# A linear-attention and mixture-of-experts layer: the expert stage's PE order built around the arriving gathers

## The reference

```python
x = L0_attn_x                                   # (2, 1024, 128) float32: 2048 tokens of 128
x = _layernorm(x + _L0_attn_ref(x, ...))        # linear attention, 16 heads of 8, with its own norm and residual
x = _layernorm(x + _L0_ffn_ref(x, ...))
# _L0_ffn_ref, E = 14 experts, one expert for each token:
logits = x @ router_w
assignments = argmax(logits); weights = softmax(logits)[assignment]
hid = gelu(x @ w1[e] + b1[e])                   # 128 -> 256
sel = hid @ w2[e] + b2[e]                       # 256 -> 128, only the chosen expert counts
moe_out = sel * weights
```

## Time and profile before

| | us |
|---|---|
| median of 3 runs | 109.59 |
| lowest, highest | 108.51, 110.13 |
| the profiled execution's own time | 107.97 |
| its span, first to last instruction | 106.2 |
| outside the span | 1.77 |

### The profile page before, as it was taken

One profiled execution on the slowest core, in us unless ns is written; L12 is line 12 of the kernel. 1 busy time (PEld: TensorE's weight loads), 2 busy tenths in 40 slices (PEclk: granted clock), 3 DMA queues, 4 the chain that ended last, 5 costly groups with the idle time before them and its releaser, 6 DMA issues.

```text
span 106.2 us, 2176 instructions
## 1 busy us (share of the span) xinstructions
PE 80.2 (76%) x588; PEld 68.5 (65%) x588; DVE 64.0 (60%) x258; ACT 58.4 (55%) x180; POOL 63.3 (60%) x109
## 2 busy tenths in 40 slices
PE   5729999999999697662888969998999999620000
PEld 3428698988978596441657769986997989510000
DVE  4699957785639887895001324333478887788500
ACT  0415499467559899970035537655446797804200
POOL 6747899910002396923777776750077888877770
PEclk9999999999999999975599999999999999975555
DMA  2848999600000000540688678770000011111110
GB/s 40 302 163 233 365 320 292 176 11 2 0 0 0 3 6 0 199 169 30 224 260 256 204 206 259 231 207 12 0 0 25 31 52 36 39 49 52 49 49 25
DMA packets 9674, 12.16 MB, mean 114 GB/s; under 512 B 1426, under 2 KB 7230, under 8 KB 9662
## 3 DMA queue, kind: packets, MB, share of 16 engines
q1 hardware_dynamic: 8276, 9.69, 28.2%
q0 software_dynamic: 1024, 2.11, 7.1%
q10 hardware_dynamic: 362, 0.23, 1.1%
HBM read 6.07 MB, written 2.11 MB: 77 GB/s over the span
## 4 chain that ended last, share of the span: by engine, by line
PE 34%; POOL 19%; DVE 13%; DMA 12%; issue 10%; ACT 5%; ACTq 2%; POOLq 1%; DVEq 0%
POOL out L529 11%; DMA acc<-x_rows,source 8%; PE ps_q L1015 7%; PE ps_a L1015 6%; PE ps_o L1015 6%; POOL acc L510 5%; DMA vec_rows<-L_ffn_b 4%; PE ps_r L1015 4%; PE ps_k L1015 4%; POOL rstd L382 3%; PE ps_t L1025 3%; ACT hid L692 2%; DVE acc L965 1%; POOLq L70 1%; ACT k_parts L697 1%
## 5 line engine op out<-in xcount | busy, mean ns | idle before, releaser
L510 POOL DMA_INDIRECT acc<-x_rows,source x16 | 16.2, 1014 | 8.7 <-DVE source L894 3.8
L965 DVE SCALAR_TENSOR_TENSOR acc<-ps_o,share,acc 128x128 f32 x29 | 10.2, 351 | 17.7 <-PE ps_o L1015 15.6
L1015 PE MATMUL ps_o<-w_sb,hid 128*128 x116 | 19.3, 289 | 1.1 <-ACT hid L692 1.0
L529 POOL DMA_INDIRECT out<-k_parts,source x16 | 15.9, 996 | 4.3 <-issue 3.7
L382 POOL TENSOR_TENSOR rstd<-ve,exponent 128x4 f32<-128x4 f32 (+3 forms) x14 | 12.5, 896 | 9.4 <-DVE ve L1003 7.1
L1015 PEld LDWEIGHTS ps_o<-w_sb,hid 128*128 128x128 f32 x116 | 15.3, 190 | 2.6 <-issue 2.1
L692 ACT ACTIVATE hid<-ps_q,shared 128x128 f32<-128x128 f32 x30 | 9.3, 361 | 5.5 <-PE ps_q L1015 5.5
L697 ACT ACTIVATE k_parts<-acc,shift,rstd 128x128 f32<-128x128 f32 x15 | 7.0, 488 | 8.5 <-DVE shift L987 8.4
L692 ACT ACTIVATE hid<-ps_k,shared 128x128 f32<-128x128 f32 x28 | 8.7, 361 | 5.4 <-PE ps_k L1015 4.3
L1015 PE MATMUL ps_q<-xs_t,shared 128*128 (+1 forms) x60 | 10.3, 295 | 0.4 <-ACT xs_t L687 0.4
L1015 PE MATMUL ps_k<-xs_t,shared 128*128 x56 | 9.6, 294 | 0.6 <-ACT xs_t L687 0.6
(11 more groups left out here) (205 smaller groups left out, 195.9 us busy)
## 6 DMA issues: line engine op xcount, KB each, us to landing
shared<-w_sb SPq DMA_DIRECT2D x29, 129.0 KB, 2.3
w_sb<-L_ffn_w SPq DMA_DIRECT2D x1, 1792.0 KB, 7.7
x_rows<-rows SPq DMA_DIRECT2D x4, 258.0 KB, 2.1
x_sb<-L_attn_x SPq DMA_DIRECT2D x4, 256.0 KB, 4.4
acc<-x_rows,source POOLq DMA_INDIRECT x16, 3.2
out<-k_parts,source POOLq DMA_INDIRECT x16
wqkv_sb<-L_attn_Wqkv ACTq DMA_DIRECT2D x1, 192.0 KB, 4.2
wo_sb<-L_attn_Wout SPq DMA_DIRECT2D x1, 64.0 KB, 4.9
```

What stands on the lines that cost most here:

```text
L510: pool.indirect_dma_start(acc[:, t, :], None, x1_rows, bass.IndirectOffsetOnAxis(ap=source[:, t:t + 1], axis=0), bounds_check=last_token, ...
L529: pool.indirect_dma_start(out_rows, bass.IndirectOffsetOnAxis(ap=source[:, t:t + 1], axis=0), res[:, t, :], None, bounds_check=last_token, ...
L965: dve.scalar_tensor_tensor(out=tile, in0=ps_y[j % 2], scalar=share[:].rearrange("p t e -> p (t e)")[:, bass.ds(t_of[j] * ROW + j, 1)], in1 ...
L1015: return pe.matmul(o, l, r, start=start, stop=stop)
```

## The change

PE's order becomes, for tile k: turn k, output of step k-2, hidden of step k. ACT copies a tile ahead of the gelu of the step before it. The fillers ahead of the stage go from 18 to 12, and `owned()` moves behind the register load on DVE. The last tiles (14 and 15) and the steps after them are written out.

```diff
@@ scalar
             tile_t(0)
-            gelu(0, 0)
-            tile_t(1)
-            tile_t(2)
             for j in range(NP):
-                if j + 1 < NP:
-                    gelu(j + 1, (j + 1) % U)
-                if j + 3 < NT:
-                    tile_t(j + 3)
-                for t in APPLY_AFTER.get(j, ()):
+                if j < E - 1:
+                    tile_t(j + 1)
+                gelu(j, j % U)
+                if E - 1 <= j < NT - 1:
+                    tile_t(j + 1)
+                for t in APPLY_AFTER.get(j - 1, ()):
                     apply(t)
+            for t in APPLY_AFTER[NP - 1]:
+                apply(t)
@@ vector
             sources()
-            owned()
 
             dve.wait_ge(steps_ok, 2)
             t_of = tiles(dve)
+            owned()
@@ tensor
-            keep_busy(idle_r, 18)
-            turn(0)
-            hidden(0)
-            turn(1)
-            turn(2)
-            for j in range(NP):
+            keep_busy(idle_r, 12)
+            for k in range(E):
+                turn(k)
+                if k >= 2:
+                    output(k - 2)
+                hidden(k)
+            output(E - 2)
+            turn(E)
+            output(E - 1)
+            hidden(E)
+            turn(E + 1)
+            output(E)
+            hidden(E + 1)
+            for j in range(E + 1, NP):
                 if j + 1 < NP:
                     hidden(j + 1)
-                if j + 3 < NT:
-                    turn(j + 3)
                 output(j)
```

## The result

The changed kernel takes 109.28 us (median of 4 runs, 108.67 to 110.29), the kernel before 109.05 (4 runs, 107.98 to 110.13), and the ratio is 1.014 with an interval of 1.007 to 1.021. The forecast was 107.6, faster. A second comparison of the same kernel gave 1.012 (1.005 to 1.020; 109.73 of 10 runs against 108.87 of 25).

What follows compares the result with a forecast made beforehand. The end was taken to stand at a fixed distance behind POOL's power 2, set by add 16; order 1.9 plus gathers 0.3 less late landing 0.2 saves 2.0, taking 109.59 to 107.6, range 106.2 to 109.2.

Steps and rivals of the forecast that it cites:

- A step without a wait takes 1.11 on PE: PE's step in the expert stage: 0.11 turn, 0.50 output, 0.50 hidden, read from the profile before.
- Turn 13 at 70.48 as before: Start of the forecast's chain on PE: turn 13 unmoved, then copy until 71.05 and hidden 13 at 71.09.
- The forecast's list of signs: What the profile after would show if right: add 16 near 77.8, POOL idle about 1 us ahead of power 2.
- Order, 1.9: PE's new order: two outputs and one hidden pass ahead of the last gather, add 16 earlier by 1.9, lower bound 1.5.
- The gelus take half back: Rival: late landing on gather 13 or 14, or a longer hidden, gelu, output chain; 108.4, chance 0.2.
- The gathers, +0.33: POOL's gather 11 and the four behind it start 0.33 earlier as copy 7 comes sooner; gain 0 to 0.33.
- Late landing: A gather landing about 4 us after issue may fall on gather 13 or 14; 0.2 taken off, bounds 0 and 0.9.
- Fillers, 0: Six fewer fillers ahead of the stage let turn 0 start at 52.9, not 53.85, hidden by the gathers; worth 0.
- the rival of a falling clock: Rival: PE's short gaps and fewer fillers lower the granted clock between 60 and 70 us; 110.2, chance 0.06.
- `owned()` on DVE, 0, and gather 0: `owned()` behind the load ends between 51.8 and 52.9, costing DVE 0; gather 0 gains 0, bounds 0 and 0.67.
- The 0.67 of the rival: Rival: POOL was held by `owned()`, so gather 0 and all others start 0.67 earlier; 106.9, chance 0.15.
- POOL stays last: Tail: POOL remains last to be ready, smallest slack 0.8 at power 5, so the 2.0 carry on to the end.

Runs made afterwards that it cites:

- e1: Changed kernel with hidden's wait for the copied tile moved onto its first matrix instruction, behind the address register work; 1.000 of before, median 108.27.
- e4: Changed kernel with each tile's hidden layer one turn later (turn k, hidden k-1, output k-2); 0.991 of before, 108.52.
- e10: Changed kernel with hidden one turn later and the address work ahead of the copy wait, on chip 2; 0.980 of before, 107.08.
- e11: Changed kernel with POOL waiting for the copy of tile t-6 instead of t-4, on chip 2; 1.005 of before, 108.93.
- e5: e1 with hidden 15 ahead of output 14, on chip 7; 0.999 of before, 113.72 against 114.1.
- e2: Kernel before, old order, with 12 fillers for 18 and `owned()` behind the register load; 0.988 of before.
- e14: Same kernel as e2 measured a second time, 12 runs; 1.000 of before, 109.09 against 109.02.
- e12: Kernel before with 28 instead of 16 warm-up matmuls at its start, on chip 2; 0.982 of before, median 108.61 against 108.87.
- e3: Changed order alone: changed kernel with 18 fillers and `owned()` ahead of the load; 1.018 of before, 109.35.
- e8: Changed kernel with POOL waiting for the copy of tile t-6 instead of t-4, on chip 7; 1.030 of before.
- e15: Same kernel as e10, hidden one turn later and early address, on chip 9; 0.993 of before.

## Why the prediction was wrong

**The step that failed: "A step without a wait takes 1.11 on PE", and with it "Turn 13 at 70.48 as before".** The 1.11 was measured in an order in which each hidden layer had its copy long before. In the new order a step contains turn, copy, address and hidden layer one after the other, 0.31 + 0.27 + 0.25 + 0.54 = 1.37. The forecast had this chain in its hand for turn 13 (copy until 71.05, hidden at 71.09) and did not ask whether it holds for every step. Asking would not have been enough: by its own numbers the chain closes in 0.57 + 0.04 + 0.50 = 1.11, below the 1.30 of the gathers. The term that it had wrong is the hand-over from copy to hidden, taken as 0.04 and measured as 0.25 (to the first matrix instruction); with 0.09 in its place (e1) the step is 1.17 and PE catches up again. A gather comes every 1.30, so a PE that needs 1.37 never catches up once gather 5 has made it late; at 1.11 it would have. From turn 6 to turn 13 it took 9.56 (before 8.51), and from gather 0 to turn 13 22.15 (before 20.85). e1 shortens the loop's address part by 0.16 and seven steps by 1.32; e4 and e10 take the copy out of it, and seven steps take 8.08 and 7.65; e11 takes the gathers' waits for recent copies out and leaves 9.55. These runs show the loop as the cause of the late turn 13. The longer waits behind turn 13, below, are read from the timeline; of them only the exchange in e5 was tried.

The distance from the forecast, add 16 at 77.99 (79.99 less 2.0), to the measured 80.72 is 2.73: 0.28 for the later start, 1.43 for turn 13 beyond that (forecast 70.35 with the gathers' 0.33 and the 0.2 for the late landing, measured 72.06; 1.05 of it is the slower pace from turn 6 to turn 13), and 1.13 behind turn 13 (8.66 for a forecast 7.53), less the 0.1 by which the sum took 1.9 for 1.98 (and roundings). The forecast's list of signs puts add 16 near 77.8, its sum at 77.99.

- *Order, 1.9.* The part that was meant to be gained is there and is small. Turn 13 to add 16 took 9.51 before and 8.66 after: 0.85 gained, where the same pieces were forecast to gain 1.98. The hand-overs were set too low: output 13 came 2.33 behind turn 13 (forecast 2.00; 0.21 of the 0.33 is the address), and each hidden, gelu and output 2.09 and 2.18 (forecast 1.89), since a PE that has just waited needs 0.60 to 0.66 to the next piece instead of 0.50. Output 15 to add 16 were 0.3 more. "The gelus take half back" had this mechanism right; taken alone it would have left a gain.
- *The gathers, +0.33.* Gather 11 came 1.36 behind gather 10 (64.71 and 63.35), not 1.30, because it follows the copies, which follow the loop. Nothing gained.
- *Late landing.* It fell on gather 5 (4.29), the last took 2.86. The text called a late gather ahead of tile 11 harmless; it was not, since at 1.37 a delay is never made good.
- *Fillers, 0.* Right: turn 0 was 0.48 earlier, and gather 5's landing took that back; e2 and e14 together show no worth. The clock stayed full from 54 us to 95, and the rival of a falling clock did not occur in this profile's stage; it did in e14's (57.2 to 60.6), in the old order with 12 fillers.
- *`owned()` on DVE, 0, and gather 0.* Right: it ended at 52.08, gather 0 landed at 52.81. The 0.67 of the rival counts from a start of gather 0 at 48.96 that no row shows. DVE and POOL at the start, after the earlier trace rows:

```profile
48.84 0.17 DVE L894 CAST source<-ps_a 128x16 int32<-128x16 f32 x1 [0.28 <-PE ps_a L1015]
...
49.91 1.28 POOL L510 DMA_INDIRECT acc<-x_rows,source  x1 [3.79 <-DVE source L894]
...
51.26 0.39 DVE L898 TENSOR_TENSOR after_b<-begin_i,slot_no 128x224 f32<-128x224 int32 x1 [2.25 <-issue]
51.49 1.03 POOL L510 DMA_INDIRECT acc<-x_rows,source  x1 [0.30 <-issue]
...
52.91 0.23 DVE L956 TENSOR_SCALAR share<-owner,acc 128x14 f32<-128x14 f32 x1 [0.83 <-DMA acc<-x_rows,source]
```

  Gather 0 starts 0.90 behind `source` with `owned()` out of the way, as it did with it, and the first indirect DMA is again 1.28 long. By the Trainium skill ("SBUF — State Buffer", section "Who interferes with whom") a VectorE instruction with two SBUF inputs contends with a GpSimd instruction that reads SBUF; gather 1, which now runs beside both operations of `owned()` (51.26 to 52.08), takes 1.03 instead of 1.00, so at most 0.03 is seen of it, and the rival built on it is out. In the other profiles with `owned()` in the new place gather 1 takes 1.00 to 1.02.
- *POOL stays last.* Right. From power 2 on, after:

```profile
78.65 0.58 POOL L382 TENSOR_TENSOR rstd<-ve,exponent 128x1 f32<-128x1 f32 x1 [0.60 <-DVE ve L1003]
...
81.91 0.73 POOL L382 TENSOR_TENSOR rstd<-ve,exponent 128x2 f32<-128x2 f32 x1 [1.40 <-DVE ve L1003]
...
103.02 0.97 POOL L529 DMA_INDIRECT out<-k_parts,source  x1 [0.30 <-issue]
```

  Add 16 to the last store's start is 22.30 (before 22.33, and 22.28 to 22.36 in every profile of chips 2 and 6). POOL's idle time ahead of power 2 grew to 1.40 where 1 was forecast, and for the opposite reason: power 2 was late, at 81.91 for 81.19.

What the forecast offered as the one slower case, a fall of the clock, was the wrong mechanism. The one that came, a loop across two engines longer than the gap between arriving tiles, was not among the rivals, though the earlier trace rows held its parts but one: the address work behind the wait.

## What to carry to other kernels

When work is moved closer to its input, don't carry over the old time of a step: write down the loop that the new order closes (producer, copy, address, consumer, next producer), add it up, and compare it with the gap between arrivals. If the loop is longer, one late arrival is never made good, and the difference is added at each step left. Take the hand-overs from a row in which the engine did wait: one that was read where nothing waited, 0.04 here, can hide work that a wait brings out, 0.25. One step of distance between a copy and its use opens the loop, and a wait put on the matrix instruction itself rather than ahead of its register work takes the address out of it.

## What the runs showed of the hardware

- Register work on PE is not free behind a semaphore: MOVE and FUSED_REGOPS put 0.24 between the end of the copy and the weight load (0.05 when they had been done before, in e1). A row shows this only as "issue".
- The first indirect DMA of the stage starts 0.9 behind its release and lasts 1.28 to 1.29, the following ones 0.99 to 1.03, in each of the eighteen profiles.
- Some gathers take 4 us or more to land instead of 3. Five transfers of 16 KB are on the page's queue "q8 instruction"; in the raw records one is at 59.1 and one at 71.7 before (gathers 6 and 15 late), at 58.1 and 72.9 after (gather 5 late; gather 15 not). In most profiles the gather in flight at such a transfer is the late one, but e12 and e2 also had late ones without, so that this is a correlation, not a cause.
- The granted clock can be at its lower level at the start of the kernel too. In the profile of the changed kernel's second comparison it was from 8 to about 15 us (stretch, PE, PEld, DVE, ACT and POOL busy with counts, then the clock, DMA share and GB/s), in after it was not:

```profile
5.00:8.00 3.00, 0.88 (x7) 0.82 (x8) 2.86 (x20) 0.58 (x2) 1.32 (x2) 1.00 0.46 167
8.00:15.00 7.00, 6.32 (x24) 4.56 (x24) 6.16 (x30) 3.50 (x11) 5.77 (x14) 0.53 0.97 315
```

```profile
8.00:15.00 7.00, 6.66 (x33) 5.29 (x33) 5.98 (x30) 3.96 (x13) 5.91 (x14) 1.00 1.01 313
```

  What PE did in the 3 us ahead was about the same (0.88 busy and 0.78). Gather 0 then started at 50.87 instead of 49.91; the profiles of e3 and e12 show the same, with 50.64 and 50.82. It goes with a good part of the spread between runs of one kernel: of the 25 runs of before beside e1, the eight with a mean granted clock of 0.881 to 0.888 took 109.0 to 110.0, the 13 with 0.906 to 0.918 took 106.8 to 109.6, on average 1.4 less.
- On chips 7 and 9 ACT stands still for 2.5 to 4.1 us (6.3 in e8) early in the stage, and DVE with it, although what they wait for is done. In e15 the copy of tile 5 starts 3.13 after the engine's last work, and the profile names only "remote":

```profile
60.17 0.27 ACT L687 COPY xs_t<-ps_r 128x128 f32<-128x128 f32 x1 [3.13 <-remote]
...
60.35 0.35 DVE L965 SCALAR_TENSOR_TENSOR acc<-ps_o,share,acc 128x128 f32 x1 [7.30 <-remote]
```

  The expert stage holds all that these chips are slower by: gather 0 to add 16 takes 33.37 in e15 and 28.90 in e10, the same kernel on chip 2, and their spans are 109.3 and 104.8. The stand-still of 3.13 is the larger part of it; right behind it, from 60.1 to 63.6, the granted clock was at its lower level. What holds the engines wasn't found.
